# Counting out-degrees with signs taken on ScalarE instead of one-hot rows compared on VectorE

## What is computed

```python
deg = jax.ops.segment_sum(jnp.ones(row.shape), row, num_segments=n)   # row = src, then one loop per node
norm = 1.0 / jnp.sqrt(deg[row] * deg[col])
```

## Time and profile before

| | us |
|---|---|
| median of three runs | 4607.52 |
| profiled execution | 4609.34 |
| its span | 4607.6 |
| DVE busy | 4012.2 (87%) |
| PE busy | 3896.1 (85%) |
| ACT busy | 2196.3 (48%) |
| sort, level 1 | 41 to 463.2 |
| sort, levels 2 and 3 | 463.2 to 1390 |

### The profile page before, as it was taken

One profiled execution on the slowest core, in us unless ns is written; L12 is line 12 of the kernel. 1 busy time (PEld: TensorE's weight loads), 2 busy tenths in 40 slices (PEclk: granted clock), 3 DMA queues, 4 the chain that ended last, 5 costly groups with the idle time before them and its releaser, 6 DMA issues. The chain is left out here.

```text
span 4607.6 us, 106894 instructions
## 1 busy us (share of the span) xinstructions
PE 3896.1 (85%) x44112; PEld 3490.5 (76%) x44113; DVE 4012.2 (87%) x6579; ACT 2196.3 (48%) x3936; POOL 237.3 (5%) x165
## 2 busy tenths in 40 slices
PE   3666666666668999995999999997999999979998
PEld 3555555555556666663999999997999999968988
DVE  8999999999998899986999999998666666668888
ACT  2222333333334555552333333333888888857776
POOL 1000001010100000000101110101000000000000
PEclk9899889888879999997999999998999999989999
DMA  3000000000002222221000000000333333300000
GB/s 104 1 1 1 1 1 1 1 1 1 1 1 109 113 113 110 113 110 44 2 2 2 2 2 2 2 2 6 110 96 99 99 97 97 98 12 5 9 10 9
DMA packets 92941, 183.53 MB, mean 40 GB/s; under 512 B 10329, under 2 KB 63781, under 8 KB 92322
## 3 DMA queue, kind: packets, MB, share of 16 engines
q1 hardware_dynamic: 91970, 174.17, 11.6%
q10 hardware_dynamic: 480, 2.40, 0.2%
HBM read 88.63 MB, written 87.90 MB: 38 GB/s over the span
## 5 line engine op out<-in xcount | busy, mean ns | idle before, releaser
L1699 ACT ACTIVATE gC<-qC 128x768 fp32r<-128x768 f32 (+3 forms) x1184 | 981.4, 829 | 802.5 <-PE qC L1740 640.3
L87 DVE TENSOR_TENSOR g<-iota_own,recs 128x768 bf16<-128x768 bf16 (+1 forms) x1200 | 636.4, 560 | 177.0 <-PE qC L1744 171.0
L1846 PE MATMUL qO<-Xr,gC 128*128 128x258 f32 (+1 forms) x4900 | 754.2, 291 | 7.8 <-ACT gC L1699 7.7
L461 PE MATMUL pV<-VO,PM 128*128 128x98 bf16 (+4 forms) x6524 | 400.9, 230 | 409.7 <-issue 404.5
L461 PEld LDWEIGHTS pV<-VO,PM 128*128 128x128 bf16 x6524 | 370.2, 111 | 436.2 <-issue 434.4
L1846 PEld LDWEIGHTS qO<-Xr,gC 128*128 128x128 f32 x4900 | 639.3, 190 | 15.7 <-ACT gC L1699 10.6
L1846 PE MATMUL qO<-A,gC 128*128 128x132 f32 x4900 | 637.2, 281 | 0.0
L1846 PEld LDWEIGHTS qO<-A,gC 128*128 128x128 f32 x4900 | 581.4, 191 | 0.0
L93 DVE TENSOR_TENSOR g<-iota_own,recs 128x1536 bf16<-128x1536 bf16 (+1 forms) x522 | 510.7, 988 | 63.4 <-PE qC L1744 48.3
L1844 PE MATMUL qO<-terms,ring 128*128 128x384 bf16 x2450 | 524.2, 327 | 0.0
L1841 PE MATMUL qO<-terms 128*128 128x64 bf16 x2450 | 470.4, 193 | 0.0
(11 more groups left out here) (248 smaller groups left out, 5709.0 us busy)
## 6 DMA issues: line engine op xcount, KB each, us to landing
sl_f<-tables SPq DMA_DIRECT2D x350, 192.0 KB, 2.3
tables<-ring SPq DMA_DIRECT2D x150, 384.0 KB, 2.3
tables<-ring SPq DMA_DIRECT2D x50, 416.0 KB, 2.4
sl_f<-tables SPq DMA_DIRECT2D x50, 224.0 KB, 2.5
edges<-terms SPq DMA_DIRECT2D x1, 4312.0 KB, 13.4
B<-in_x SPq DMA_DIRECT2D x1, 2744.0 KB
out<-B SPq DMA_DIRECT2D x7, 392.0 KB
terms<-in_edge_type ACTq DMA_DIRECT2D x2, 686.0 KB
```

The lines of the kernel that those rows point to most:

```text
L87: return v.tensor_tensor(o.rearrange("p n (a b) -> p n a b", b=2), (iota_own if own else iota_b)[:, at:at + w].rearrange("p (a b) -> p a b ...
L461: mm = pe.matmul(pV[n % 2][:, g * row:(g + 1) * row].rearrange("p (f b) -> p f b", f=u.nf), PM[:, n % 2, col, :], values[:, :, col, :], st ...
L1699: act.activation(Cs[:, u % 2, 0:n, :], pC[u % 2][:, 0:n, :], ACT.Copy).then_inc(s_cs, 1)
L1846: mm = pe.matmul(pO[i % SUMS][:, 0:width], table_j, x, start=first, stop=last)
```

## The change

The source place is no longer compared for equality. A sign function of (i - place - 0.5) over i = 0 to 128 is -1 up to the place and +1 beyond it; summed over the edges of a tile it gives a curve whose neighbouring differences are twice the count of edges at that place.

- Two ACT copies are added to the preparation: `turn_at` (-place - 0.5, float32) and `ts_p` (the source tile of every column, each value twice, bf16). Both lie in unused ends of `recs`.
- ACT writes `side`: ten sign activations of 129 elements in each of units 0 to 156 (eight in the last), after V(n+2), with a column of `turn_at` as a bias pointer.
- DVE writes `ts_hot`, ten columns of 50, after PM(n) in units 0 to 156. The four `out_hot` comparisons of units 0 to 48 are gone.
- PE multiplies `ts_hot` and `side` of unit n-1 after route(n): ten matmuls of 129 columns instead of 32 of 128, in 157 units instead of 49.
- The degree steps move from unit 73 to unit 161 and after; one subtraction of neighbours is added, and the scale 0.5.
- V(n) does not wait for `out_hot` any more.

The first `sources` in the diff is on PE, the second on DVE, behind PM(n).

```diff
+            turn_at = recs[:, :, :].rearrange("p c w -> p (c w)")[:, RC * 4 - COLS:RC * 4]
+            ts_p = recs_h.rearrange("p c h -> p (c h)")[:, RC * 8 - 4 * COLS:RC * 8 - 2 * COLS].rearrange("p (c b) -> p c b", b=2)
...
-            out_hot = sb("out_hot", [P, 2, 16, NTE + P + 2], BF16, c1)
+            side = sb("side", [P, 2, 16, P + 2], BF16, c1)
+            ts_hot = sb("ts_hot", [P, 2, 16, NTE], BF16, c1)
...
+            SIDES = 10
+            COUNTED = -(-COLS // SIDES)
+            pieces_of = {n: (n * SIDES, min(SIDES, COLS - n * SIDES)) for n in range(COUNTED)}
...
                     act.activation(edges[:, F_W, :], ew, ACT.Copy).then_inc(weighed, 1)
+                    act.activation(turn_at, psrc, ACT.Copy, bias=-0.5, scale=-1.0).then_inc(fields, 1)
+                    act.activation(ts_p, twice(esrc, COLS), ACT.Copy).then_inc(fields, 1)
...
                         if n >= 3:
                             act.wait_ge(s_val, n - 2)
-                            act.wait_ge(s_outhot, 2 * min(n - 2, A_N))
...
+                    def sides(n):
+
+                        at, cols = pieces_of[n]
+                        if n >= 2:
+                            act.wait_ge(s_outadd, n - 1)
+                        for j in range(cols):
+                            ins = act.activation(side[:, n % 2, j, 0:P + 1], iota_b[:, 0:P + 1], ACT.Sign, bias=turn_at[:, at + j:at + j + 1])
+                        ins.then_inc(s_side, 1)
...
                             if n + 2 < b:
                                 double(n + 2)
+                            if n in pieces_of:
+                                sides(n)
...
                     def sources(n):
-                        for h in range(2):
-                            pe.wait_ge(s_outhot, 2 * n + h + 1)
-                            for k in range(16):
-                                mm = pe.matmul(pD[0:NT, 0:P], out_hot[:, h, k, 0:NT], out_hot[:, h, k, NTE + 1:NTE + 1 + P], start=n + h + k == 0,
-                                               stop=n == A_N - 1 and h == 1 and k == 15, skip_group_check=True)
-                            mm.then_inc(s_outadd, 1)
+                        at, cols = pieces_of[n]
+                        pe.wait_ge(s_outhot, n + 1)
+                        pe.wait_ge(s_side, n + 1)
+                        for j in range(cols):
+                            mm = pe.matmul(pD[0:NT, 0:P + 1], ts_hot[:, n % 2, j, 0:NT], side[:, n % 2, j, 0:P + 1], start=at + j == 0,
+                                           stop=at + j == COLS - 1, skip_group_check=True)
+                        mm.then_inc(s_outadd, 1)
...
                             route(n)
-                            if n < A_N:
-                                sources(n)
+                            if 1 <= n <= COUNTED:
+                                sources(n - 1)
...
-                        if n == A_N + 20 + 4:
-                            v.wait_ge(s_outadd, 2 * A_N)
-                            v.tensor_copy(dego[:, :], pD[0:NT, 0:P]).then_inc(s_deg, 1)
+                        if n == COUNTED + 4:
+                            v.wait_ge(s_outadd, COUNTED)
+                            v.tensor_copy(degx[:, :], pD[0:NT, 0:P + 1]).then_inc(s_dego, 1)
+                            v.wait_ge(s_dego, 1)
+                            v.tensor_tensor(dego[:, :], degx[:, 1:P + 1], degx[:, 0:P], ALU.subtract).then_inc(s_deg, 1)
...
                     def sources(n):
-                        for h in range(2):
-                            if n >= 1:
-                                v.wait_ge(s_outadd, 2 * n + h - 1)
-                            for at, w, field in ((0, NTE, F_TS), (NTE, P + 2, F_SL)):
-                                codes = fields_of(n)[:, field, h * 16:(h + 1) * 16, :]
-                                ins = equal(v, out_hot[:, h, :, at:at + w], codes, 16, w)
-                            ins.then_inc(s_outhot, 1)
+                        at, cols = pieces_of[n]
+                        if n >= 2:
+                            v.wait_ge(s_outadd, n - 1)
+                        equal(v, ts_hot[:, n % 2, 0:cols, :], ts_p[:, at:at + cols, :], cols, NTE).then_inc(s_outhot, 1)
```

More of the change, by code:

```diff
@@ L157, in gnn_four_layers_kernel @@
             ew_r = PM[:, :, :, :].rearrange("p h n w -> p (h n w)")[:, 0:2 * COLS].bitcast(F32)
-            out_hot = sb("out_hot", [P, 2, 16, NTE + P + 2], BF16, c1)
+            side = sb("side", [P, 2, 16, P + 2], BF16, c1)
+            ts_hot = sb("ts_hot", [P, 2, 16, NTE], BF16, c1)
             dego = sb("dego", [NT, P], F32, c1)
+            degx = sb("degx", [NT, P + 1], F32, c1)
             degs = sb("degs", [P, NT], F32, c1)
@@ L162, in gnn_four_layers_kernel @@
             total_of = sb("total_of", [P, 1], F32, c1)
-            junk = out_hot[:, :, :, :].rearrange("p h n w -> p (h n w)")
+            junk = side[:, :, :, :].rearrange("p h n w -> p (h n w)")
             WT = sb("WT0", [P, 2, P], F32, c1)
@@ L178, in gnn_four_layers_kernel @@
                      "s_dup", "s_hot", "s_cnt", "s_look", "s_mul", "s_rank", "s_more", "s_pair", "s_val", "s_perm", "s_out", "s_ev",
-                     "s_outhot", "s_outadd", "s_deg", "s_tp0", "s_xt0", "s_y0", "s_lin0", "s_link0", "s_wt0", "s_valid", "s_total", "s_kind")
+                     "s_outhot", "s_side", "s_dego", "s_outadd", "s_deg", "s_tp0", "s_xt0", "s_y0", "s_lin0", "s_link0", "s_wt0", "s_valid", "s_total", "s_kind")
             (loads, pads, consts, tri_made, prep, fields, blanks, weighed, s_pad, s_load, s_xin, s_stored, turned, wt_made,
              s_dup, s_hot, s_cnt, s_look, s_mul, s_rank, s_more, s_pair, s_val, s_perm, s_out, s_ev,
-             s_outhot, s_outadd, s_deg, s_tp, s_xt, s_y, s_lin, s_link, s_wt, s_valid, s_total, s_kind) = [sem(n, c1) for n in names]
+             s_outhot, s_side, s_dego, s_outadd, s_deg, s_tp, s_xt, s_y, s_lin, s_link, s_wt, s_valid, s_total, s_kind) = [sem(n, c1) for n in names]
             ends = [sem(f"ends{i}", c1) for i in range(2)]
@@ L207, in gnn_four_layers_kernel @@
             phases = [(0, A_N), (A_N, UN)]
+            SIDES = 10
+            COUNTED = -(-COLS // SIDES)
+            pieces_of = {n: (n * SIDES, min(SIDES, COLS - n * SIDES)) for n in range(COUNTED)}
             done_with = {u.d: n + 1 for n, u in enumerate(units) if u.level == 3}
+            assert COUNTED < done_with[7] and 8 * TOP * NX * 8 <= RC * 8 - 4 * COLS
             LIN, LIN_AT = 7, A_N + 28
             assert LIN_AT + 3 * NT + 1 <= UN
-            PREP, FIELDS, WEIGHED = 15, 7, 4
+            PREP, FIELDS, WEIGHED = 15, 9, 4
             PADDED = 96
@@ L423, in _ @@
                                 double(n + 2)
+                            if n in pieces_of:
+                                sides(n)
                             if n == A_N - 8:
                                 weights_turned()
-                            if n == A_N + 20 + 14:
+                            if n == COUNTED + 14:
                                 act.wait_ge(s_deg, 4)
@@ L499, in _ @@
                                 mm.then_inc(s_y, 1)
-                            if n == A_N + 20 + 8:
+                            if n == COUNTED + 8:
                                 pe.wait_ge(s_deg, 1)
@@ L617, in degrees @@
                     def degrees(n):
-                        if n == A_N + 20 + 4:
-                            v.wait_ge(s_outadd, 2 * A_N)
-                            v.tensor_copy(dego[:, :], pD[0:NT, 0:P]).then_inc(s_deg, 1)
-                        if n == A_N + 20 + 11:
+                        if n == COUNTED + 4:
[3 more added lines that the diff above has]
+                            v.tensor_tensor(dego[:, :], degx[:, 1:P + 1], degx[:, 0:P], ALU.subtract).then_inc(s_deg, 1)
+                        if n == COUNTED + 11:
                             v.wait_ge(s_deg, 2)
-                            v.tensor_scalar(degs[:, :], pW[:, P:P + NT], 1.0, None, ALU.add).then_inc(s_deg, 2)
-                        if n == A_N + 20 + 18:
+                            v.tensor_scalar(degs[:, :], pW[:, P:P + NT], 0.5, 1.0, ALU.mult, ALU.add).then_inc(s_deg, 2)
+                        if n == COUNTED + 18:
                             v.wait_ge(s_deg, 5)
```

## The result

The changed kernel takes 4525.72 us (median of 4 runs, 4522.79 to 4534.1) against 4607.05 before: a ratio of 0.9826, 95% interval 0.9813 to 0.9839. That is 81 us faster; 90 were forecast, and the time lies in the range.

What follows compares the result with a forecast made beforehand. DVE was taken to bound the sort: -160.2 + 52.6 + 0.3 + 2.4 + 15 = -89.9 us, from the profiled 4609.3 to 4519.4, less 1.8 for the median, so 4518 us, range 4493 to 4562.

Steps and rivals of the forecast that it cites:

- DVE is the bound of the sort: Sort: DVE has no gap in level 1, so time off DVE is kernel time; DVE's balance -107.3 us.
- -160.2 for `out_hot`, +52.6 for `ts_hot`: DVE in the sort: 49 units each lose 3.27 us of `out_hot`; 157 units each gain 0.335 us of `ts_hot`.
- The last level-1 unit gains 0.55: End of level 1: only the PE part goes, so it gains 0.55 us and not 2.94, adding +2.4.
- A sign starts 0.294 after the last: ACT: spacing of one-pointer signs from SBUF, bounds 0.254 and 0.386 us; ten take 2.94 us.
- The loop and the clock, +15, bounds 0 to 51: Two-unit loop through signs, `place`, PM: about 1 us at full clock plus 14 of 51 at TensorE's lower clock.
- The sum: Whole kernel: all terms give -89.9 us, to 4518 us, with the aggregation layers only shifted.
- What would show it: Signs listed for the sort: level-1 period 5.6 us, later near 5.5, sort's end near 1300, PM waiting much over 15.
- the first rival: Sort: all of DVE's balance arrives as low clock stretches become rarer; 4503 us, or 4484; chance 0.15.
- The rival with 0.386 us per sign: ACT closes the loop in the sort, ten signs taking 3.86 us; 4556 us, up to 4590; chance 0.20.
- low stretches: Sort: time with TensorE at its lower clock, 18% in level 1, 28% later, where the loop's PE part doubles.
- The rival with all of DVE's balance: Sort: full -107.3 us arrives, less 2.4; 4503 us, or 4484 with M's 18.6 us of waits gone; chance 0.15.
- The rule against the change: Signs on ACT: skill sends plain elementwise work to VectorE; a column costs DVE 77 ns, ACT 294; move would lose.

Runs made afterwards that it cites:

- the two-pointer run: Changed kernel with a second pointer operand (a scale of ones) in each sign, nothing computed differently: 4606.91 us, ratio 0.9999 to the kernel before.
- one matmul: Changed kernel with one degree matmul per unit instead of ten, still between route and count: 4514.33 us, ratio 0.9798 to the kernel before.
- both moves together: Changed kernel with signs split four and six around ACT's wait and degree matmuls before route: 4492.35 us, ratio 0.9753 to the kernel before.
- the second pair: Changed kernel with degree matmuls before route, ten per unit against one per unit: 4498.23 and 4504.34 us.

## Why the prediction was right, step by step

- *DVE is the bound of the sort.* Right. From 41 us to `total_of` DVE is busy 1309.1 us before and 1201.2 after, 107.9 less, where the balance said 107.3. All other versions that keep `ts_hot` have 1194.9 to 1209.5, and their sorts differ by what DVE waits for.
- *-160.2 for `out_hot`, +52.6 for `ts_hot`.* Right. Level 1 shortened by 134.9 where 48 x (3.27 - 0.335) = 140.9 was its share before waits, and leaving out the counting in 156 units gave 157.1 us at the end of the sort (1389.03 to 1231.96), against 160.2 - 0.3 - 2.7 - 0.3 = 156.9 by the same terms (with no `ts_hot` in it, the last level-1 unit gives back 3.27 - 0.55 = 2.7).
- *The last level-1 unit gains 0.55.* It gained 9.56 - 9.03 = 0.53.
- *A sign starts 0.294 after the last.* 0.293. The value came from two neighbouring rows and a difference of 92 ns per pointer; this held, and the two-pointer run gave the other row's number too.
- *The loop and the clock, +15, bounds 0 to 51.* What is left over is 6.0 in level 1 (140.9 - 134.9) and 52.1 - 36.2 - 0.3 = 15.6 later, 21.6 together, so the term was about 7 too small. The part that it described came as forecast: PM waits 15.2 us for `place`. That its size fits so well is partly luck, for the 14 of 51 was chosen with no row behind the share. The other part was put at nothing: more waits of M for R. Without the one at unit 49 (2.6 before, 2.1 after) they went from 17.9 to 23.8, as the ten matmuls now stand between route and count in levels 2 and 3 too. All of M's waits are 25.9 us here, 16.6 with one matmul and 11.6 with the matmuls before route. The length of the loop was right: from the start of route to the start of the count the sum had 1.43 + 0.60 = 2.03, and the trace has 705.80 - 703.74 = 2.06.
- *The sum.* -104.9 + 21.6 = -83.3 is what the sort shows, and 4525.7 - 4607.05 = -81.3 the medians. 90 were forecast. The layers were taken to be only shifted; in the profiled executions they took 8.1 us more, which the sum did not have.
- *What would show it.* Level-1 periods of 5.59 in units without waits (5.6 forecast); 5.63 in units 49 to 156, from 335.05 to 943.25 (near 5.5); the sort's end at 1305.7 (near 1300); the granted clock of levels 2 and 3 at 0.88 against 0.86 before, so hardly a sign of the first rival. PM's 15.2 us of waits is no proof of the loop by the prediction's own mark (much over 15); the runs with one sign per unit and with the signs split are.
- *The rival with 0.386 us per sign* (4556, up to 4590) was wrong in its price: it takes 4606.9. It had put more waits in the low stretches, but not that they would become longer, and in level 1 the clock fell from 0.91 to 0.78. Had that been the sign's spacing, the range would have missed.
- *The rival with all of DVE's balance* (4503, or 4484 with M's waits gone too) is not what the change does, but both moves together land between its two numbers: 4492. Its reason was rarer low stretches of the clock; this version gets there mainly by the shorter loop, though its clock is higher as well (0.94 against 0.90 in 320 to 940 us). The rule of the Trainium skill (TensorE: Matmul & The Clock Gate, The two states you'll see) that the clock follows activity is borne out in direction, 0.85 to 0.90 and 0.87 to 0.92 with more matmuls per unit. In the second pair, with the place kept, that was worth 6 us net; most of the waits went by taking signs and matmuls out of the loop.
- *The rule against the change* (the Trainium skill, ScalarE: Activation LUTs, Rules for kernel authors) has its per-element price confirmed: 293 ns for a column of signs on ACT against 77 on DVE. The kernel is faster all the same, because DVE was the full engine; at 388 ns per column the gain is gone.

## What to carry to other kernels

Work moved from the full engine to an idle one is not free because the idle one has the time. Look at what stands behind it in that engine's order, add up the loop that closes through it over as many units as it spans (two here), and put the work where the engine waits anyway: the same ten signs cost 20 us less when split around a wait, the same ten matmuls 31 us less in PE's gap.

When such a loop is within some per cent of the bounding engine's own time (4.94 and 5.37 us by the prediction's sum), a small price can decide everything. Here 95 ns more per sign, 1568 times, took the whole gain, along with a lower granted clock in level 1. Look for such a shift in every stage, not in one window: between 320 and 940 us the clock had hardly moved.

An instruction that is added to the full engine need not cost its whole time, when that engine also has waits: count them before and after.

## What I had not expected of the hardware

- Ten activations that were each 0.388 - 0.293 = 0.095 us longer (the price of a second pointer operand, as the rows had said) came with a granted clock of TensorE of 0.78 instead of 0.91 in level 1, though PE's own work was the same.
- A single matmul between two groups whose records otherwise overlap costs 0.26 us of the chain (from -0.16 to +0.10), though each of the other nine adds only (0.63 - 0.10) / 9 = 0.06. Whether that is its waits or something else was not tested.
- Taking matmuls out lowered the granted clock (0.90 to 0.85, 0.92 to 0.87), so that a version with less work on PE ran its other matmuls at a lower mean clock.
- The same step at the start of the last layer had a mean granted clock of 0.60 before and 0.51 after, some 2670 us behind the sort and in code that the change does not touch; the time between its first and last row grew from 17.78 to 22.00 us.
